# Linear attention with the flow sums' heads on partitions, in four column groups of TensorE, and the projections put between the links of the chain

## The reference, cut to what matters

```python
def _L1_attn_ref(x, Wq, bq, Wk, bk, Wv, bv, Wo, bo):
    ...
    q = jax.nn.sigmoid(proj(Wq, bq))
    k = jax.nn.sigmoid(proj(Wk, bk))
    v = proj(Wv, bv)
    sink_incoming = 1.0 / jnp.einsum('nhld,nhd->nhl', q + EPS, k.sum(axis=2) + EPS)
    source_outgoing = 1.0 / jnp.einsum('nhld,nhd->nhl', k + EPS, q.sum(axis=2) + EPS)
    conserved_sink = jnp.einsum('nhld,nhd->nhl', q + EPS, (k * source_outgoing[..., None]).sum(axis=2) + EPS)
    conserved_source = jnp.einsum('nhld,nhd->nhl', k + EPS, (q * sink_incoming[..., None]).sum(axis=2) + EPS)
    conserved_source = jnp.clip(conserved_source, -1.0, 1.0)
    sink_allocation = jax.nn.sigmoid(conserved_sink * (float(l) / float(s)))
    source_competition = jax.nn.softmax(conserved_source, axis=-1) * float(s)
    kv = jnp.einsum('nhld,nhlm->nhdm', k, v * source_competition[..., None])
    out = jnp.einsum('nhld,nhdm->nhlm', q * sink_incoming[..., None], kv)
    out = out * sink_allocation[..., None]
    ...
    return out @ Wo.T + bo
```

## Time and profile before

| | |
|---|---|
| median of 3 runs | 2208.47 us (2199.37 to 2210.56) |
| profiled execution | 2208.38 us, its span 2206.4 us |
| busy, share of the span | PE 88%, PEld 66%, DVE 65%, ACT 45%, POOL 42% |
| stretch of linear attention | 938 to 1257 us of the span |

### The profile page before, as it was taken

How to read it: one execution, slowest core, us unless ns; L and a number is a source line. 1 busy time by engine, 2 the same in 40 slices (tenths; PEclk the granted TensorE clock), 3 DMA queues, 4 the chain that set the end, 5 groups by cost and what they waited for, 6 DMA issues and landing times. The chain is left out here.

```text
span 2206.4 us, 60606 instructions
## 1 busy us (share of the span) xinstructions
PE 1934.4 (88%) x21423; PEld 1458.4 (66%) x21426; DVE 1438.6 (65%) x3456; ACT 988.2 (45%) x1977; POOL 937.7 (42%) x978
## 2 busy tenths in 40 slices
PE   6999997997999489929999779999999999984675
PEld 3666666886888467728888657666767667652333
DVE  3666664775777634426676546776767777754998
ACT  2444442443111033413453335555555555534997
POOL 0111111221577723345655135656565565632333
PEclk8999997998999689968999879999999999985555
DMA  6211004995222199733331101101010101000111
GB/s 199 82 33 33 28 29 162 329 329 202 61 52 53 32 279 299 234 96 98 102 98 62 41 29 35 33 29 37 25 37 26 35 26 35 21 9 28 57 57 43
DMA packets 157099, 192.84 MB, mean 87 GB/s; under 512 B 27971, under 2 KB 140614, under 8 KB 157013
## 3 DMA queue, kind: packets, MB, share of 16 engines
q1 hardware_dynamic: 146741, 189.09, 27.3%
q0 software_dynamic: 10272, 2.62, 0.6%
HBM read 140.81 MB, written 77.51 MB: 99 GB/s over the span
## 5 line engine op out<-in xcount | busy, mean ns | idle before, releaser
L2960 DVE TENSOR_REDUCE xa_kq<-xa_A 100x4 f32<-100x1444 f32 x128 | 212.6, 1661 | 158.4 <-PE xa_A L2629 158.4
L2788 ACT ACTIVATE xa_prob<-xa_A 121x1600 f32<-121x1600 f32 x96 | 144.5, 1505 | 234.5 <-PE xa_A L2656 234.5
L2863 POOL TENSOR_TENSOR xa_prob<-xa_prob,xa_exp_bias 121x1600 f32<-121x1600 f32 x64 | 228.9, 3576 | 41.0 <-ACT xa_prob L2788 41.0
L1425 POOL DMA_INDIRECT slot_rows<-rt_x_again,rt_slot_u x150 | 155.2, 1035 | 67.7 <-issue 63.1
L2656 PEld LDWEIGHTS xa_A<-xa_q2T,xa_kqT 17*121 17x121 f32 x3072 | 92.3, 184 | 46.8 <-issue 29.7
L2888 POOL TENSOR_TENSOR xa_o_rstd<-xa_o_var,xa_power 100x1 f32<-100x1 f32 x32 | 17.8, 557 | 240.6 <-DVE xa_o_var L3000 240.6
L2629 PE MATMUL xa_A<-xa_kqT 16*100 16x361 f32 x1024 | 113.0, 511 | 6.8 <-ACT xa_prob L2788 6.8
L1671 POOL DMA_INDIRECT contrib<-ex_y,ex_place_u x64 | 62.4, 975 | 119.9 <-ACT ex_y L1723 107.1
L2656 PE MATMUL xa_A<-xa_q2T,xa_kqT 17*121 17x100 f32 x3072 | 108.5, 278 | 4.8 <-DVE xa_kq L2960 4.2
L717 DVE TENSOR_TENSOR sa_masked<-sa_A,sa_later_keys 100x1600 f32<-100x1600 f32 x32 | 58.4, 1824 | 73.1 <-PE sa_A L471 73.1
L2573 PE MATMUL xa_C<-xa_wk,xa_rows_T 128*121 128x256 f32 x384 | 103.7, 408 | 1.7 <-ACT xa_rows_T L2768 1.7
(11 more groups left out here) (353 smaller groups left out, 5115.9 us busy)
## 6 DMA issues: line engine op xcount, KB each, us to landing
ex_w<-in_w13T SPq DMA_DIRECT2D x64, 352.0 KB, 8.6
contrib<-xs_zero SPq DMA_DIRECT2D x30, 640.0 KB, 6.6
la_rows<-contrib SPq DMA_DIRECT2D x16, 1200.0 KB
xs_ctxT<-in_ctxT SPq DMA_DIRECT2D x32, 512.0 KB
xa_rows_t<-in_ctx SPq DMA_DIRECT2D x96, 121.0 KB
ex_w<-in_w2T SPq DMA_DIRECT2D x64, 176.0 KB
slot_rows<-xs_zero SPq DMA_DIRECT2D x32, 272.0 KB, 4.3
ex_x_t<-slot_rows SPq DMA_DIRECT2D x64, 136.0 KB, 6.1
```

The lines of the kernel that those rows point to most:

```text
L1425: nc.gpsimd.indirect_dma_start(slot_rows, bass.IndirectOffsetOnAxis(slot_u[:, k, n:n + 1], 0), x_again[:, k, :], None, bounds_check=SLOTS ...
L2788: nc.scalar.activation(prob[:, n, :].rearrange("p (h a) -> p h a", h=HPG), A[:ROWS, :, 0:G * T], ACT.Exp, scale=EXP_SCALE).then_inc(exp_re ...
L2863: nc.gpsimd.tensor_tensor(chunk, chunk, exp_bias[:, n, :].unsqueeze(1).to_broadcast([ROWS, HEADS, T]), ALU.mult).then_inc(biased, 1)
L2960: nc.vector.tensor_reduce(kq[:T, k, NCH, 4 * j:4 * j + 4, DH:DH + 1].rearrange("p h o -> p (h o)"), A[:T, :, 0:src_len], axis=AXIS_X, op=A ...
```

## The change

It does five things in `linear_attention`.

1. The flow sums change their layout. `against` takes the weights, 32 columns, as stationary operand and moves the 100 tokens; the result has heads on partitions. There are four kinds of sums (of keys or queries, for either sequence of the unit), each goes to 32 output partitions of its own and so to a column group of TensorE (`group`). `weighted_sums` does the same with 256 moving columns and 4 matmuls in place of 8, `keys_values` makes 16 products of 32x32 (a group for each pair of heads) in place of 4 of 128x128.
2. What must lie with tokens on partitions again is turned back: `turn_inverse`, `turn_sums`, `turn_shares` are four transposes, and ACT copies two of the results out of PSUM (`inverse_out`, `sums_out`).
3. The softmax runs along the free axis: exp leaves its sum (`accum_out`), DVE inverts 64 values, ACT scales. `sum_exponentials` is gone.
4. PE's queue has another order: the four projections of unit b+1 and the two halves of `project_out` stand between the links of the chain.
5. `keep` moves from DVE to POOL, the sum with the epsilon of the norm too (`roots`); POOL's roots stand behind its sums from b = 2 on. On ACT `normalise` stands ahead of `y_out` and `tokens_out`, and `finish`, now of unit b-4, early in the body. One body more is at the end.

One table of 128x256 more is loaded with the stage's weights (`own_dims`).

```diff
-        DEN, AB, CONS, ESUM = 0, 64, 320, 384
+        DEN, INV, OWN = 0, T, T + P
+        TURNED, CONS, SHARES = 0, D, D + T
+        SUMS, SUMS_E = OWN + D, OWN + D + 4 * KC
+        KEY, QUERY = 0, 1
...
-        FIRST, LAST, REACH = -3, 3, 4
+        FIRST, LAST, REACH = -3, 4, 4
...
+        def group(of, two):
+            return slice(2 * HEADS * (2 * of + two), 2 * HEADS * (2 * of + two) + 2 * HEADS)
+
...
+                def keep(b):
+                    k = b[1] % 2
...
+                    pool.wait_ge(x3_ready, at(b, 1, 1))
+                    pool.wait_ge(r_ready, at(later(b, -2), 1, 1))
+                    nc.gpsimd.tensor_tensor(x_bo[:, k], x_3[:, k], bo[:].unsqueeze(1).to_broadcast([T, 2, D]), ALU.add).then_inc(kept, 1)
...
                 def body(b, has):
-                    if has(2) or has(-3):
+                    if b[1] < 2 and (has(2) or has(-3)):
                         roots(b, has)
                     if has(3):
                         of = slice(0, 1 if b[1] == FIRST else 2)
                         add_halves(later(b, 3), of)
                         add_rows(later(b, 3), of)
+                    if b[1] >= 2 and (has(2) or has(-3)):
+                        roots(b, has)
+                    if has(0):
+                        keep(b)
...
+                        pe.wait_ge(r_ready, at(later(b, -3), 1, 1))
...
+                def against(b, column, weights, sums_of_other):
+                    k = b[1] % 2
+                    for c in range(KC):
+                        for of in (KEY, QUERY):
+                            for two in range(2):
+                                columns = group(1 - of if sums_of_other else of, two)
+                                last = nc.tensor.matmul(X[5][group(of, two), column:column + T], weights[:, c, columns],
+                                                        qke[:, k, place(of, c), two * T:(two + 1) * T], start=(c == 0), stop=(c == KC - 1))
+                    return last
...
+                    pe.wait_ge(wt1_ready, at(b, 1, 1))
+                    pe.wait_ge(qke_ready, at(b, 1, 1))
+                    pe.wait_ge(vc_ready, at(later(b, -1), 1, 1))
+                    pe.wait_ge(g_ready, at(later(b, -1), 1, 1))
+                    against(b, DEN, wt1, False).then_inc(den_done, 1)
...
+                def turn_inverse(b):
+                    pe.wait_ge(inverted, at(b, 1, 1))
+                    nc.tensor.transpose(X[5][:T, INV:INV + P], inv_h[:], ident[:]).then_inc(inv_turned, 1)
...
+                def keys_values(b):
+                    k = b[1] % 2
+                    pe.wait_ge(vc_ready, at(b, 1, 1))
+                    pe.wait_ge(yT_ready, at(later(b, -1), 1, 1))
+                    for two in range(2):
+                        for c in range(KC):
+                            for h in range(GROUPS):
+                                n, o = two * KC + c, c * P + 32 * h
+                                last = nc.tensor.matmul(X[6][32 * h:32 * h + 32, 32 * n:32 * n + 32], tok[:, k, two, D + o:D + o + 32],
+                                                        v[:, k, two, o:o + 32], start=True, stop=True)
+                    last.then_inc(kv_done, 1)
...
+                def weighted_sums(b):
+                    k = b[1] % 2
+                    pe.wait_ge(inv_ready, at(b, 1, 1))
+                    pe.wait_ge(tok_ready, at(b, 2, 2))
+                    for of in (KEY, QUERY):
+                        for two in range(2):
+                            last = nc.tensor.matmul(X[5][group(of, two), OWN:OWN + D], inv[:, k, group(of, two)],
+                                                    tok[:, k, two, (1 - of) * D:(2 - of) * D], start=True, stop=True)
+                    last.then_inc(own_done, 1)
...
+                def turn_sums(b):
+                    pe.wait_ge(own_ready, at(b, 1, 1))
+                    for c in range(KC):
+                        last = nc.tensor.transpose(X[5][:, TURNED + c * P:TURNED + (c + 1) * P], own_sums[:, c * P:(c + 1) * P], ident[:])
+                    last.then_inc(own_turned, 1)
...
+                def conserved(b):
+                    pe.wait_ge(wt2_ready, at(b, 1, 1))
+                    against(b, CONS, wt2, True).then_inc(cons_done, 1)
...
+                def turn_shares(b):
+                    pe.wait_ge(comp_ready, at(b, 1, 1))
+                    pe.wait_ge(alloc_ready, at(b, 1, 1))
+                    nc.tensor.transpose(X[5][:T, SHARES:SHARES + P], shares[:], ident[:]).then_inc(shares_turned, 1)
...
+                def project_out(b, two):
+                    if two == 0:
+                        pe.wait_ge(yT_ready, at(b, 1, 1))
+                        pe.wait_ge(r_ready, at(later(b, -1), 1, 1))
+                        if b[1] + 2 < NU:
+                            pe.wait_ge(tok_ready, at(later(b, 2), 2, 1))
+                    for c in range(KC):
+                        last = nc.tensor.matmul(X[4][:T, two * D:(two + 1) * D], yT[:, c, two * T:(two + 1) * T], wo[:, c, :],
+                                                start=(c == 0), stop=(c == KC - 1))
+                    if two == 1:
+                        last.then_inc(o_done, 1)
...
                     if coming:
                         turn_rows(later(b, 1))
...
+                    if now:
+                        denominators(b)
+                    if prev:
+                        keys_values(later(b, -1))
+                    if now:
+                        turn_inverse(b)
+                    if coming:
+                        project(later(b, 1), 0)
+                    if now:
+                        weighted_sums(b)
+                    if coming:
+                        project(later(b, 1), 1)
+                    if now:
+                        turn_sums(b)
+                    if coming:
+                        project(later(b, 1), 2)
+                    if now:
+                        conserved(b)
+                    if coming:
+                        project(later(b, 1), 3)
...
+                        project_out(later(b, -2), 0)
                     if now:
-                        sum_exponentials(b)
+                        turn_shares(b)
+                    if has(-2):
+                        project_out(later(b, -2), 1)
+                    if prev:
+                        attend(later(b, -1))
+                    if coming:
+                        turn_qk(later(b, 1), 0)
+                        turn_qk(later(b, 1), 1)
                     if prev:
                         turn_y(later(b, -1))
                     if coming:
                         values(later(b, 1))
-                        turn_qk(later(b, 1), 0)
-                        turn_qk(later(b, 1), 1)
...
+                    k = b[1] % 2
+                    act.wait_ge(inv_turned, at(b, 1, 1))
+                    act.wait_ge(own_done, at(later(b, -2), 1, 1))
+                    act.wait_ge(g_ready, at(later(b, -2), 1, 1))
+                    nc.scalar.activation(inv[:, k, :], X[5][:T, INV:INV + P], ACT.Copy).then_inc(inv_ready, 1)
...
+                    act.wait_ge(own_turned, at(b, 1, 1))
+                    act.wait_ge(cons_done, at(later(b, -1), 1, 1))
+                    nc.scalar.activation(wt2[:].rearrange("p c n -> p (c n)"), X[5][:, TURNED:TURNED + KC * P], ACT.Copy).then_inc(wt2_ready, 1)
...
+                    nc.scalar.activation(ecs[:], clipped[:], ACT.Exp, accum_out=esum[:]).then_inc(ecs_ready, 1)
+                    act.wait_ge(shares_turned, at(later(b, -1), 1, 1))
+                    nc.scalar.activation(shares[LINES // 2:LINES, :], X[5][LINES // 2:LINES, CONS:CONS + T], ACT.Tanh, scale=0.5).then_inc(alloc_ready, 1)
+                    act.wait_ge(rec_ready, at(b, 1, 1))
+                    nc.scalar.activation(shares[0:LINES // 2, :], ecs[:], ACT.Copy, scale=rec[:]).then_inc(comp_ready, 1)
...
                         rows_out(later(b, 1))
                     if has(0):
+                        inverse_out(b)
+                    if has(-4):
+                        finish(later(b, -4))
+                    if has(0):
+                        sums_out(b)
+                    if has(1):
+                        gates(later(b, 1), 0)
+                    if has(0):
...
+                        gates(later(b, 1), 1)
                         gates_e(later(b, 1))
+                    if has(2):
+                        normalise(later(b, 2))
                     if has(-1):
                         y_out(later(b, -1))
                     if has(1):
                         tokens_out(later(b, 1), 0)
                         tokens_out(later(b, 1), 1)
-                    if has(0):
-                        raise_allocation(b)
-                    if has(2):
-                        normalise(later(b, 2))
-                    if has(-3):
-                        finish(later(b, -3))
...
+                    dve.wait_ge(inv_turned, at(later(b, -1), 1, 1))
```

(26 more changed lines are left out.)

291 lines of the change are left out of this document (103 added, 188 removed).

## The result

The changed kernel takes 2186.12 us (median of 6 runs, 2180.83 to 2193.16) against 2206.36 for the kernel before (6 runs on the same chip, 2199.37 to 2212.87): a ratio of 0.991 (95% interval 0.988 to 0.994), 20 us faster. Six more runs later gave 0.989 (0.986 to 0.991). The forecast was 2167, 41 us.

A forecast was written before the change was run, and what follows sets the result against it. PE's queue bound the loop; the links would bind next. 14 x (15.74 - 13.2) = 35.6, plus 8.5 for start, body 0 and end, less 3 for low clock: 41 off 2208.4, 2167 us (2157 to 2178; 8 in 10: 2150 to 2188).

The forecast's parts named there:

- body 0: The first body of linear attention, 18.5 us before; forecast 3 us shorter (bounds 1 and 6) through less PE work.
- the end: Stretch behind the last body's start, 22.5 us of bare chain with shorter products; forecast 3 us off (bounds -1 and 5).
- the start: Ahead of the first chain, where two `first_weights` instructions took 3.56 us; forecast saving 2.5 us (bounds 0 and 3.2).
- the 3 us set aside for a lowered clock in the loop: Taken off the forecast saving for one stretch at the low clock, as before, since 13.2 a body holds none.
- one such stretch: Low clock in the earlier kernel's loop, 1058 to 1070 at a mean of 0.72; priced at 3.4 us.
- behind POOL's roots, now at the end of its body: Where `normalise`, SP's 200 KB load and the second sum queue; that ring was priced at 11.7 us, under 13.2.
- The ring of 13.2: Loop wait expected to bind: `residual`, `keep` on POOL, `normalise`, `y_out`, `tokens_out`, next `turn_rows`; 13.2 us a body.
- Rival 1: PE still bounds the loop, the ring through `keep` being shorter: 12.4 us a body, 2153 us; 12%.
- Rival 2: Links between engines are longer, about 0.25 us more at each of four places: 14.3 a body, 2183 us; 17%.
- four places: Links that might each take about 0.25 us more, among them reciprocal, exp with its sum, ACT busy with gates.
- Rival 3: Column groups don't run beside each other on PE: 16.5 us a body, 2210 us, no change; 4%.
- Rival 4: PE's clock falls in the loop through more waits, transposes and smaller products: 18 us a body, 2232 us; 5%.

The follow-up runs named there:

- the spare products: Changed kernel plus 16 matmuls per body ahead of `keys_values`, results unread: 8 on the column groups of `against`, 8 on one group; 2203.8 us, 1 run.

## Why the prediction was right in kind and wrong by half

The forecast saved 41 us, the stage saved 22.4. By the prediction's own terms, in us of saving missed: body 0, 5.3; body 1 to 2, 9.5; body 2 to 3, 2.3; twelve bodies of 0.32, 3.9; the end 1.7 (21.2 in place of 22.5, forecast 3 off). In its favour: the start, 3.4 saved where 2.5 were counted, and the 3 us set aside for a lowered clock in the loop, which didn't occur. That the clock stayed up there was luck, not forecast. The prediction read one such stretch in the kernel before where there were two, of 3.1 us each. The misses add up to 22.7, and less the 3.9 in favour they make 18.8, against 18.6 to be explained (41 - 22.4).

**The step that failed: POOL's order in bodies 0 and 1, taken as that of the loop.** The prediction says "behind POOL's roots, now at the end of its body"; that is so from body 2 on. In bodies 0 and 1 the roots stayed ahead and only `keep` went to the end. The prediction asked what stands behind a new wait on ACT in the loop and not in these two bodies, where the sums of 7.4 us stand between the roots and `keep`. So body 0, counted as 3 us shorter, grew from 18.5 to 20.8, and body 1 to 2, counted as 13.2, grew from 14.3 to 22.7: 14.8 us of the saving that was missed. Shown from both sides: `keep` ahead of the sums gives 14.1 us back, roots behind them 11.3.

**The ring of 13.2: it exists, but it is one of three and not the one that binds.** Keep's ring exists and is what is left when the others are open (12.93 with `y_out` out of it, and 0.51 less with a faster `keep`). With its `y_out` of 0.45 it would be about 13.4, worked out and not measured alone: 0.2 more than priced. But two rings through `attend` stood beside it and hold the loop at 13.57: one is closed by `turn_qk` in PE's own queue, the other goes on through ACT's queue to `turn_rows`. The prediction priced `attend` and didn't ask who waits for it: in the kernel before it lay early in PE's body, here it is directly ahead of `turn_qk`, and the qk copy between the two was guarded by it all along. PE's idle time was forecast at `turn_rows` (0.5) and is at `turn_qk` (1.04). The error in the body, 0.32, is small only because the three rings lie so close: that is luck.

**What held.** PE's work per body is 11.9 (12.4 forecast); `against` 0.37 to 0.48 (0.5); weighted sums 0.57 (0.6); the reciprocal 0.78 (0.82); `keep` 1.27, ended by residual (1.3); no DVE instruction over 1 us (the reduction, the longest, takes 0.99). `keys_values` took 0.48, below its lower bound of 0.5, so PE idles 0.61 behind the reciprocal where 0.2 to 0.3 were expected. The Trainium skill (TensorEngine Tiling (Array Packing), Key Properties) says that a change of tiling mode drains the engine. Here no more than about 0.1 us of it shows: `against` takes 0.37 to the next start where the column-grouped `keys_values` follows and 0.48 where a projection does. No run isolates it. All grouped products together stayed below their prices, which held 0.25 us for start-up.

**Rivals.** Rival 1 did not happen: PE is busy 87% of the loop. Rival 2's size came near (25 us) but not by its mechanism: neither `turn_sums` nor `turn_shares` waits in the loop, and of its four places the reciprocal alone shows as idle time of PE, 0.61 behind it. Rival 3 is ruled out by the spare products. Rival 4 did not happen in the changed kernel's loop (clock 1.00), but the clock was low in bodies 1 and 2, behind the long waits, and in the loops of several variants. Two of its readings of the kernel before do not hold: the low stretch around 992 to 1007 began at 988.8, while PE stood in a wait of 6.28 us (to 992.54), and projections of 200 columns ran in it beside the products of 32.
